# Statistics of the third stage taken in the second, the seam of the second stage reordered, on one Trainium2 core

## The reference

```python
x = x + gnn(layernorm(x), adj)                  # stage 1, untouched
x = x + mamba2_block(layernorm(x), ...)         # stage 2, "state-space"
#   z, xBC, dt = split(x @ W_in);  xBC = silu(conv(xBC));  dt = softplus(dt + dt_bias)
#   A_cum = cumsum(dt * A);  Lmat = exp(A_cum[l] - A_cum[s]) for s <= l;  Y = (C B^T * Lmat) (x dt) + D x
#   Y = Y * silu(z);  Y = Y * rsqrt(mean(Y*Y) + EPS) * norm_w;  out = Y @ W_out @ W_lin + b_lin
x = x + adj_norm @ (layernorm(x) @ weight) + bias   # stage 3, "routing", first half
x = x + moe(layernorm(x))                       # stage 3 picks 2 of 8 experts a token and scatters; stage 4 computes
```

## Time and profile before

| | |
|---|---|
| median of 3 runs (lowest to highest) | 1187.71 us (1187.52 to 1189.35) |
| the profiled execution: its time, its span | 1188.17 us, 1186.4 us |
| busy, share of the span: PE / DVE / ACT / POOL | 86% / 66% / 60% / 41% |
| stage 2, from its first matmul to its last update | about 395 to 704.5 us |
| stage 3, to the last scatter | 705.5 to 869.1 us |
| stage 3, DVE's tables for stage 4 behind the last destinations | 850.0 to 861.9 us |
| stage 3, one iteration: ACT's own instructions (two weight copies of 2.5 us apart) | 4.7 us |
| stage 3, one round over L1408, L1416 on PE and L1262 on ACT, at 2.4 and at 1.2 GHz | 3.5 and 6.0 us |

### The profile page before, as it was taken

The page is one execution under the profiler, slowest core; times in us unless marked ns, Lnnn a source line. Parts: engine busy times, 40 slices in busy tenths (PEclk is TensorE's granted clock), DMA queues, the critical chain, the costliest instruction groups (busy, mean ns, idle before and its releaser), DMA issues. The chain is left out here.

```text
span 1186.4 us, 23416 instructions
## 1 busy us (share of the span) xinstructions
PE 1018.5 (86%) x6808; PEld 892.6 (75%) x6808; DVE 780.1 (66%) x2068; ACT 710.6 (60%) x1561; POOL 484.8 (41%) x482
## 2 busy tenths in 40 slices
PE   2999999999998767999999856876349999799997
PEld 1998988988987635666677655765349999799997
DVE  4587776777776756788777747799825555355554
ACT  4556556556554359999999826666125555355553
POOL 4223223223222024445555334466724444334444
PEclk9999999999999788999999987788569999899999
DMA  5131121121110023332223219162435444333331
GB/s 165 46 89 46 45 88 44 44 88 44 44 36 1 23 75 71 72 70 65 60 60 68 37 41 288 60 196 74 140 91 151 134 130 126 91 91 99 95 97 52
DMA packets 82346, 99.07 MB, mean 84 GB/s; under 512 B 9307, under 2 KB 68194, under 8 KB 82122
## 3 DMA queue, kind: packets, MB, share of 16 engines
q1 hardware_dynamic: 72058, 74.24, 23.1%
q0 software_dynamic: 8752, 21.25, 5.1%
q10 hardware_dynamic: 1440, 2.40, 0.6%
HBM read 72.23 MB, written 27.02 MB: 84 GB/s over the span
## 5 line engine op out<-in xcount | busy, mean ns | idle before, releaser
L1607 PE MATMUL e_p_y<-w,e_gT 128*128 (+1 forms) x852 | 118.2, 275 | 0.0
L1554 DVE TENSOR_TENSOR e_g<-e_sl,e_p_h 128x342 f32<-128x342 f32 x142 | 72.6, 511 | 63.3 <-ACT e_sl L1532 57.8
L1536 ACT ACTIVATE e_gT<-e_p_gx 128x384 f32<-128x384 f32 x142 | 69.8, 491 | 63.7 <-PE e_p_gx L1597 63.7
L1532 ACT ACTIVATE e_sl<-e_p_h 128x342 f32<-128x342 f32 x142 | 64.9, 457 | 69.5 <-PE e_p_h L89 69.3
L1607 PEld LDWEIGHTS e_p_y<-w,e_gT 128*128 128x128 f32 (+1 forms) x852 | 106.1, 191 | 0.4 <-issue 0.4
L1518 POOL DMA_INDIRECT sorted_scratch<-e_xg x71 | 69.2, 974 | 91.0 <-DVE e_xg L1564 88.0
L87 PE MATMUL e_p_h<-w_hi,e_xT_hi 128*128 x284 | 104.4, 368 | 1.4 <-DVE e_g L1554 0.8
L1516 POOL DMA_INDIRECT out<-e_xg x71 | 69.0, 972 | 85.7 <-DVE e_xg L1564 78.2
L875 DVE SCALAR_TENSOR_TENSOR m_c<-m_p_x,m_vecs,m_c 128x506 f32<-128x506 f32 (+2 forms) x144 | 95.5, 736 | 5.4 <-ACT m_c L786 5.4
L1558 DVE TENSOR_TENSOR e_xT_lo<-e_p_gx,e_xT_hi 128x128 fp32r<-128x128 f32 x142 | 41.4, 292 | 86.2 <-ACT e_xT_hi L1540 85.9
L763 POOL TENSOR_TENSOR m_cum<-m_cum,m_never 128x1024 f32<-128x1024 f32 x16 | 37.8, 2359 | 133.7 <-DMA m_cum<-cum_scratch 133.7
(11 more groups left out here) (357 smaller groups left out, 3368.6 us busy)
## 6 DMA issues: line engine op xcount, KB each, us to landing
e_xg<-sorted_scratch SPq DMA_DIRECT2D x142, 130.0 KB, 2.1
m_cum<-cum_scratch SPq DMA_DIRECT2D x16, 1024.0 KB, 7.9
g_adjT<-in_adjT SPq DMA_DIRECT2D x16, 512.0 KB, 3.9
g_adj<-in_adj SPq DMA_DIRECT2D x16, 512.0 KB, 5.2
c_adjT<-in_adjT SPq DMA_DIRECT2D x16, 512.0 KB, 6.6
x_tokens<-in_x SPq DMA_DIRECT2D x16, 256.0 KB, 4.9
sorted_scratch<-nothing SPq DMA_DIRECT2D x2, 1040.0 KB, 10.2
sorted_scratch<-nothing SPq DMA_DIRECT2D x12, 130.0 KB, 2.5
```

The costliest lines, as they stand in the source:

```text
L1536: act.activation(gT[:, c % D3], p_gx[i % 2][:, 0:len(CH)], ACT.Copy).then_inc(q["gT_ready"], 1)
L1554: dve.tensor_tensor(g[:, i % D3], sl[:, i % 2], p_h3[i % 2][:, 0:HP], ALU.mult).then_inc(q["g_ready"], 1)
L1607: last = pe.matmul(p_y[d % 2][:, 0:P], gT[0:r, d % D3, k], w2k[:, bass.ts(e, P)], start=k == 0, stop=k == len(CH) - 1)
```

## The change

Three things are changed.

1. At the seam in stage 2, PE does all dt rows first, then the x product of step 0 and the weight product; ACT and DVE do the dt chain and the running sums before the first taps. The `m_late` copy of step 0 alone moves from POOL to DVE, behind `m_xdt` of step 0.
2. The first statistics of stage 3 move into stage 2: DVE takes them right behind the residual update of each step and writes mean and variance into `norm`.
3. Stage 3 starts with one Ln, one Exp and five DVE instructions over all 64 tiles (`logs1` to `shift1`). After that no step waits for a first scale; the per-step set is that of the second layernorm alone, four instructions instead of five, and 16 sets instead of 19. All lags in stage 3 become one smaller; `W_STEP` stays (4, 6).

```diff
-                    for b in range(2):
+                    for b in range(2 if s else 1):
...
-                    act.wait_ge(q["masked"], 2 * (d + 1))
+                    act.wait_ge(q["masked"], 2 * d + 1)
+                    act.wait_ge(q["first_late"], 1)
...
-            later_taps(0)
             dve.wait_ge(q["abs_ready"], 1)
...
+            later_taps(0)
...
+                if d == 0:
+                    dve.wait_ge(cum_in[0], 16)
+                    rows = cum[:, 0].rearrange("p h (g b l) -> p h g b l", g=G, b=2)
+                    dve.tensor_tensor(late[:, 0], rows[:, :, :, 1], never[:].rearrange("p (a b l) -> p a b l", a=1, b=1).broadcast_to([P, HEADS, G, P]), ALU.add).then_inc(q["first_late"], 1)
...
+                    for j in range(T):
+                        dve.wait_ge(q["x_updated"], o * T + j + 1)
+                        dve.bn_stats(stats[:, j], X[:, o * T + j, :]).then_inc(q["stats_done"], 1)
+                    for j in range(T):
+                        dve.wait_ge(q["stats_done"], o * T + j + 1)
+                        dve.bn_aggr(norm[:, 1:3, o * T + j], stats[:, j]).then_inc(q["mv_done"], 1)
...
-                if i == EARLY:
-                    pe.wait_ge(q["next_loaded"], 16 * len(next_weights))
-                    x_product(0)
...
             last.then_inc(q["dt_done"], 1)
+            pe.wait_ge(q["next_loaded"], 16 * len(next_weights))
+            x_product(0)
...
-    XS, AGG, OUT = 1, 2, 3
+    XS, AGG, OUT = 0, 1, 2
...
+            act.activation(logs1[:], norm[:, 2], ACT.Ln, bias=eps[:, 0:1]).then_inc(q["logs1_done"], 1)
+            act.wait_ge(q["logs1_done"], 1)
+            act.activation(rough1[:], logs1[:], ACT.Exp, scale=-0.5).then_inc(q["rough1_done"], 1)
...
-                if live(i):
-                    statistics(lambda t: X[:, t, :], i, i, stats, 0, q["stats_done"], q["mv_done"])
```

More of the change, by code:

```diff
@@ L802, in _ @@
             act.activation(l_[:], e_[:], ACT.Ln, bias=1.0).then_inc(q["l_ready"], 1)
+            act.wait_ge(q["next_loaded"], 16 * len(next_weights))
+            first_taps(0)
+            act.wait_ge(q["w2_done"], 1)
+            for k in range(2):
+                act.activation(w_out[:, k, :], p_w2[:, k], ACT.Copy, scale=vecs[:, 15 + k:16 + k]).then_inc(q["w2_ready"], 1)
             pieces = table[:].rearrange("p (j c) k h -> p k c j h", c=2)
@@ L946, in _ @@
                         last = pe.matmul(p_dt, w_dt[:, SEQ_ROWS - HEADS * j:SEQ_ROWS - HEADS * j + P], XT[:, j * N:(j + 1) * N], start=j == 0, stop=j == BS - 1)
-                if i == EARLY:
-                    pe.wait_ge(q["next_loaded"], 16 * len(next_weights))
-                    x_product(0)
-                    for k in range(2):
-                        last = pe.matmul(p_w2[:, k], w_outT[:, k * P:(k + 1) * P], w_lin[:], start=True, stop=True)
-                    last.then_inc(q["w2_done"], 1)
-            last.then_inc(q["dt_done"], 1)
+            last.then_inc(q["dt_done"], 1)
+            pe.wait_ge(q["next_loaded"], 16 * len(next_weights))
+            x_product(0)
+            for k in range(2):
+                last = pe.matmul(p_w2[:, k], w_outT[:, k * P:(k + 1) * P], w_lin[:], start=True, stop=True)
+            last.then_inc(q["w2_done"], 1)
             pe.wait_ge(q["w2_ready"], 2)
@@ L1063, in expert_weights, with dispatch_phase @@
     return pair("w1", [P, EX, HP]), pair("w3", [P, EX, HP]), w2
[L1066 removed]
+def dispatch_phase(nc, w, X, norm, dinv, rows, source, words, filled, pad_at, nothing, experts, adjT_dram, sorted_dram, eye):
     ADJ = 5
[L1071 removed]
+    XS, AGG, OUT = 0, 1, 2
     NORM2 = OUT + 1
@@ L1263, in _ @@
                 if live(c):
-                    u = c + OUT
-                    act.wait_ge(q["shift_ready"], u + 1)
+                    act.wait_ge(q["shift_ready"], c + 1)
                     for j in range(T):
                         t = c * T + j
-                        act.activation(rows[:, t, XN:XN + P], rows[:, t, RES:RES + P], ACT.Identity, bias=shift[:, u % 2, 1, j:j + 1], scale=scale[:, u % 2, 1, j:j + 1]).then_inc(q["xn2_ready"], 1)
+                        act.activation(rows[:, t, XN:XN + P], rows[:, t, RES:RES + P], ACT.Identity, bias=shift[:, c % 2, j:j + 1], scale=scale[:, c % 2, j:j + 1]).then_inc(q["xn2_ready"], 1)
                 n, half = group(i - PICK)
@@ L1287, in then @@
                 dve.wait_ge(q["chain"], count_[0])
-            def statistics(x_of, s, i, st, k, st_done, m_done):
-                for j in range(T):
-                    dve.bn_stats(st[:, s % 2, j, :], x_of(s * T + j)).then_inc(st_done, 1)
-                for j in range(T):
-                    dve.wait_ge(st_done, T * s + j + 1)
-                    dve.bn_aggr(mv[:, i % 2, k, j, :], st[:, s % 2, j, :]).then_inc(m_done, 1)
             def wide(v):
@@ L1326, in _ @@
                                                  op0=ALU.mult, op1=ALU.add).then_inc(q["updated"], 1)
-                    dve.wait_ge(q["updated"], T * (u + 1))
-                    statistics(lambda t: rows[:, t, RES:RES + P], u, i, stats2, 1, q["stats2_done"], q["mv2_done"])
+                    need(dve, q["shift_ready"], u - 1)
+                    need(dve, q["rough_done"], u - 1)
+                    for j in range(T):
+                        dve.wait_ge(q["updated"], u * T + j + 1)
+                        dve.bn_stats(stats2[:, u % 2, j, :], rows[:, u * T + j, RES:RES + P]).then_inc(q["stats2_done"], 1)
+                    for j in range(T):
+                        dve.wait_ge(q["stats2_done"], u * T + j + 1)
+                        dve.bn_aggr(mv[:, u % 2, j, :], stats2[:, u % 2, j, :]).then_inc(q["mv2_done"], 1)
                 n, half = group(i - PICK)
```

81 lines of the change are left out of this document (36 added, 45 removed).

## The result

Four runs beside four of the kernel before: 1172.48 us median (1171.93 to 1173.16) against 1188.03, a ratio of 0.9866 (95% interval 0.9852 to 0.9881), so 15.5 us faster. The forecast was 1176.2 with a range of 1168 to 1184.5. The profiled execution took 1171.93 us with a span of 1170.1 us and a mean granted clock of 0.933 of 2.4 GHz (before 1188.17, 1186.4 and 0.929).

A forecast was written before the change was run, and what follows sets the result against it. Bound: a PE-DVE ring in stage 2; in stage 3 DVE, then POOL's scatters. Terms -4.5 + 7.2 + 1.1 + 1.1 - 8.5 - 7.9 = -11.5 us from 1188.17, less 0.46 for the median: 1176.2, range 1168 to 1184.5.

The forecast's parts named there:

- the ring: Stage 2's loop of z, transposes, `m_xdt`, taps, update, statistics, `m_y`: a round was to grow from 15.92 to 16.57 us.
- Statistics in stage 2, +7.2: Statistics on DVE ahead of `m_y` make z 0.65 us later in each of 11 iterations, +7.2 us; bounds 0 and 11.8.
- Everything behind z moves with it: output product, squares, transposes: Stage 2: the late z delays all that follows, up to the next x product, by its full 0.65 us a round.
- a sign against its term: Stage 2 in the new profile: a ring still at 15.9 us would prove the statistics term wrong.
- The rival of full cover: Stage 2: DVE's 3.31 us idle time covers the statistics, so 7.2 us less, 1169.0 us; chance 0.12.
- Drain and end, +2.2: End of stage 2: ACT's last decay factors 1.1 us later, and the last step's statistics ahead of the barrier another 1.1.
- Seam, -4.5: Start of stage 2: earlier dt chain and sums, late copy on DVE held by POOL; -4.5 us, bounds -2 and -6.
- First scatter, -8.5: Stage 3 up to POOL's first scatter: fewer DVE waits bring it from 768.79 to 760.3; bounds -5 and -12.
- Scatter gaps, -7.9: Stage 3 from the first scatter: four gaps of 2.45 us shrink to 0.4 to 0.5; -7.9 us, bounds -4 and -9.5.
- POOL becomes the bound, gaps nearly vanish: Stage 3 scatters: DVE's pair of iterations falls to 12.7 us, below POOL's own 12.75.
- The rival with another bound in stage 3: Stage 3: PE at half clock limits first, first scatter gains 5 and gaps 4 us; 1183.6 us, chance 0.24.
- the clock fall in the ring: Stage 2 rival: added PE idleness drops the clock to 1.2 GHz, 4.5 us more per such iteration; slower, chance 0.06.

The follow-up runs named there:

- E7: Changed kernel with both weight splits one step earlier, W_STEP (3, 5) for (4, 6); 1184.42 us on a second, slower chip, ratio 0.9868 to the kernel before.
- F1: The changed kernel run again unaltered, on a third chip; 1172.19 us, ratio 0.9879 to the kernel before.
- E5: Changed kernel with the four first statistics of each step computed twice, ahead of `m_y`; 1194.77 us on the second chip, ratio 0.9947 to the kernel before.
- E2: Changed kernel with the old seam, so only statistics in stage 2 and the new stage 3; 1177.13 us, ratio 0.9922 to the kernel before.
- E1: Kernel before with the seam's part of the change alone; 1183.67 us, ratio 0.9964 to the kernel before.
- E8: Changed kernel with the late copy of step 0 back on POOL; 1179.87 us on the second chip, ratio 0.9824 to the kernel before.
- F2: Changed kernel with the statistics behind the next iteration's W products and step 0's late copy back on POOL; 1166.51 us, ratio 0.9837 to the kernel before.
- E4: Changed kernel with POOL adding the bias into the residual rows for all steps ahead of the first scatter; 1166.19 us, ratio 0.9822 to the kernel before.
- F3: F2 with all sixteen bias adds done by POOL ahead of the first scatter, in rows; 1160.98 us, ratio 0.9782 to the kernel before.

## Why the prediction was right, and where not

The number came near in part because errors went both ways: the ring was 5.6 us too dear, and between profiles of the same stage 2 the fill differs by 3.8 us (E7, F1) and the drain by 1.8, with the granted clock. That the seam's term and the sum came so near is partly luck.

*Statistics in stage 2, +7.2.* This is the step that failed by most. That z comes 0.65 us late was exact. The step that failed is the sentence "Everything behind z moves with it: output product, squares, transposes". The squares did not: PE waited for ACT's `m_zs` ahead of them already, and 0.51 of 0.65 fell into that. Measured 0.145 a round, +1.6, and a ring of 16.05 us is nearer to the 15.9 that the prediction itself called a sign against its term than to its 16.5. The rival of full cover was nearer in this term, but not in the reason: DVE's idle time covers nothing, as E5 shows with each further 0.77 us in full. The row was to be had: L994's wait for ACT's `m_zs` stands in the waits of PE's loads from 480 to 670 us, 7.0 us in twelve times.

*Drain and end, +2.2.* Measured +2.1 in F1 and in E2, and there by the two parts forecast: the last round 14.92 us in place of 13.84, the last statistics 1.06. In the first profile it is +3.9; 1.6 of the difference stand in rows at the lower clock.

*Seam, -4.5.* Measured -5.0, and the same in E1, but -4.0 in F1 and -7.8 in E7, where the second x product ran at 0.51 and at full clock. E7 lies outside the bounds of -2 to -6, so how near the first profile came to -4.5 was luck. The late copy behaved as said: held until POOL's instruction ended (2.72 us). What was not asked is whether POOL would have been sooner with its own: by E8 and F2 it is, by about 2.4 us at the decay factors and 1.8 to 1.9 in the fill, in every profile in which the second x product ran below full clock; at full clock (E7) DVE's copy took 1.37 us and was over before POOL could have ended its own (432.79 + 2.35).

*First scatter, -8.5.* Measured -9.6. The picks did run beside the second split, for 4.2 us and not 3, and E7 shows no cheap way out.

*Scatter gaps, -7.9.* Measured -6.9. The claim that failed is "POOL becomes the bound, gaps nearly vanish". It took the 15.2 us of DVE's pair for work. They held a wait already, in a row of the kernel before that was not read (timeline of DVE; the adds are at 779.06 for 2.50 us):

```profile
779.75 1.84 DVE L1360 SCALAR_TENSOR_TENSOR c_den<-c_z,c_e 128x8 f32<-128x8 f32 x1
```

It takes 0.17 us when free. Eight instructions follow it on the way to the destinations, and they made every gap 2.45 us long: the gap began with the end of POOL's adds (781.56) as this instruction's release did. Lightened by 2.5 us, DVE met the adds with its cast, the last but one instruction of that way, and the gap was 0.92. So a gap's size was set by what stands behind the held instruction, and not by either engine's load. E8, on the second chip, bears this out by chance: DVE stood still for 0.4 to 1.0 us there, and other instructions met the adds (timeline of DVE).

```profile
765.46 3.03 DVE L1360 COPY rows<-c_gate 128x8 f32<-128x8 f32 x1
779.59 3.14 DVE L1357 SCALAR_TENSOR_TENSOR c_den<-c_z,c_e 128x8 f32<-128x8 f32 x1 [0.99 <-DVE c_z L1356]
```

POOL waited 1.81 us where the copy was held, with five instructions behind it, and 2.47 us where `c_den` was, as in the kernel before. Without the lock a pair takes 10.95 us (E4), near 15.05 - 1.67 - 2.5 = 10.9 from the old rows.

The Trainium skill, "SBUF — State Buffer", section "Who interferes with whom", has the shared port pair as an exclusive lock for a whole instruction, and lists casts among the instructions that can take it. The cast was held by POOL's adds, which agrees. It was also held in the last 0.42 us of a scatter's issue (768.34 to 768.76), and by it alone for 0.43 us in E4. In the length the measurement goes beyond what the page says: a lock of one instruction gives at most 1.27 us beside an add, and 2.6 us behind two and 5.0 behind four were measured.

*The sum.* The medians lie 3.7 us from the forecast, the profiles 4.8: 5.6 from the ring, 1.1 each from the first scatter and from stage 1, 0.5 from the seam, less 1.0 (gaps), 1.7 (drain) and 0.8 (stage 4). The rival with another bound in stage 3 did not come, though PE's clock in the window was 0.79; nor did the clock fall in the ring (0.99).

## What to carry to other kernels

Work on a ring costs what it delays the first instruction that nobody else delays already: before adding up a lateness over the rounds, follow it to the next wait behind it and subtract. On DVE and POOL a gap may be a lock and no load; look for a tiny instruction with a long duration just ahead of the wait, and lay the other engine's long instructions where this one waits anyway. And when work is handed to an engine to relieve another, ask when each of the two could start.

## What the runs showed of the hardware

A small DVE instruction with two inputs in SBUF can be held across several POOL instructions in a row: 4.98 and 5.00 us beside four adds of 1.25 (E4, F3), though beside another such row one got in behind each add (1.19 us each, both runs), and beside the weight split behind each of POOL's instructions (0.83 us each). Casts and copies of 8 or 16 columns were held as well (2.98 us in the changed kernel, 3.03 in E8). No `BATCH_NORM_STATS2` and no update from PSUM was held in any run (at most 0.30 and 0.35 us each). TensorE's clock after the same gap of 2.8 us at the seam was granted at 1.00 in one run (E7), 0.67 in the first profile and 0.51 in F1, all with the same stage 2: the x product took 2.81, 4.51 and 5.46 us. The profiles of the drain differ by up to 1.8 us in the same way.
